# A decoder's fourth norm taken by groups inside the self-attention loop before it, and the first gate group of its feed-forward in halves

## The reference, cut to what matters

```python
def _layernorm(x):                       # no gain, no bias
    return (x - mean(x)) / sqrt(var(x) + 1e-5)

x = x + L0_attn(_layernorm(x));  x = x + L0_xattn(_layernorm(x), ctx);  x = x + L0_ffn(_layernorm(x))
x = x + L1_attn(_layernorm(x))           # 16 heads of 16, relative bias, causal; "second self-attention"
x = x + L1_xattn(_layernorm(x), ctx)     # one head of 256, masked; its norm is "norm 2" here
x = x + L1_ffn(_layernorm(x))

def L1_ffn(x):
    x = act_qdq(x)                       # to 16 bits by the largest |x| of the whole tensor
    up = act_qdq(x @ W_up.T)
    gate = act_qdq(x @ W_gate.T)         # needs the largest |gate| of all 768 x 1600 values first
    sig = fixed_qdq_u16(sigmoid(gate))
    gate = act_qdq(gate * sig)
    return act_qdq(gate * up) @ W_down.T
```

## Time and profile before

| | us |
|---|---|
| median of 3 runs (lowest, highest) | 1400.14 (1398.1, 1403.7) |
| the profiled execution, whole | 1396.8 |
| its span, first to last instruction | 1395.0 |
| PE busy in the span | 1245.3 |
| DVE busy | 1002.9 |
| ACT busy | 748.8 |
| POOL busy | 247.2 |

### The profile page before, as it was taken

The page is one execution under the profiler, slowest core; times in us unless marked ns, Lnnn a source line. Parts: engine busy times, 40 slices in busy tenths (PEclk is TensorE's granted clock), DMA queues, the critical chain, the costliest instruction groups (busy, mean ns, idle before and its releaser), DMA issues.

```text
span 1395.0 us, 27628 instructions
## 1 busy us (share of the span) xinstructions
PE 1245.3 (89%) x9826; PEld 1067.9 (77%) x9826; DVE 1002.9 (72%) x2488; ACT 748.8 (54%) x1769; POOL 247.2 (18%) x330
## 2 busy tenths in 40 slices
PE   5999999979999999999999999999889979979418
PEld 4889989868788777878877788777667756769418
DVE  5975777555677777777777777777689974675984
ACT  5653535354655565555565555565456644425862
POOL 2433323334000000000000000000054433210100
PEclk9999999989999999999999999999999988989859
DMA  9200001041000000000000000000020012300001
GB/s 283 69 1 24 24 3 44 1 165 36 12 1 13 12 12 11 11 0 11 12 11 11 11 0 12 11 1 1 1 61 2 3 47 76 99 26 0 1 0 48
DMA packets 34547, 40.65 MB, mean 29 GB/s; under 512 B 4889, under 2 KB 29066, under 8 KB 34442
## 3 DMA queue, kind: packets, MB, share of 16 engines
q1 hardware_dynamic: 33614, 39.24, 9.1%
q10 hardware_dynamic: 828, 0.14, 0.1%
HBM read 35.36 MB, written 4.01 MB: 28 GB/s over the span
## 4 chain that ended last, share of the span: by engine, by line
PE 52%; DVE 16%; issue 6%; ACT 4%; POOL 1%; DVEq 0%; ACTq 0%; POOLq 0%
PE bank L780 8%; PE bank L782 7%; PE bank L781 7%; PE bank L1003 4%; PE bank L993 3%; PE bank L985 3%; PE bank L961 3%; ACT prob L1679 2%; DVE nmx L2335 2%; DVE amax L2526 2%; PE bank L1237 2%; PE bank L1255 2%; DVE kTl L2106 2%; PE bank L1365 2%; PE bank L1327 1%
## 5 line engine op out<-in xcount | busy, mean ns | idle before, releaser
L1679 ACT ACTIVATE prob<-bank,nmx 100x361 f32<-100x361 f32 x256 | 142.4, 559 | 203.3 <-DVE nmx L2335 199.2
L2335 DVE TENSOR_REDUCE nmx<-bank 100x1 f32<-100x361 f32 x256 | 124.1, 526 | 62.7 <-PE bank L985 61.7
L694 POOL TENSOR_TENSOR frstd<-fmoments,eps 100x1 f32<-100x1 f32 x32 | 6.2, 192 | 645.0 <-DVE fmoments L2278 645.0
L780 PE MATMUL bank<-cxTh,wxkh 128*128 128x362 f32 x256 | 99.9, 390 | 9.4 <-DVE kTl L2106 8.2
L2352 DVE TENSOR_SCALAR prob<-prob,rsum 100x361 f32<-100x361 f32 x256 | 92.9, 405 | 4.5
L993 PE MATMUL bank<-ident,prob 100*128 100x100 f32 (+1 forms) x768 | 89.6, 252 | 0.6 <-DVE prob L2352 0.5
L993 PEld LDWEIGHTS bank<-ident,prob 100*128 100x128 f32 (+1 forms) x768 | 84.5, 151 | 6.2 <-DVE prob L2352 2.0
L780 PE MATMUL bank<-wxvh,cxTh 128*128 128x512 f32 (+1 forms) x192 | 84.5, 440 | 2.0 <-DVE vv L2258 1.6
L782 PE MATMUL bank<-cxTh,wxkl 128*128 128x362 f32 x256 | 84.1, 329 | 0.0
L781 PE MATMUL bank<-cxTl,wxkh 128*128 128x362 f32 x256 | 83.8, 327 | 0.0
L1003 PE MATMUL bank<-pT,vv 128*64 128x100 f32 (+1 forms) x1536 | 81.5, 255 | 1.7 <-ACT pT L1673 0.6
(11 more groups left out here) (428 smaller groups left out, 3686.5 us busy)
## 6 DMA issues: line engine op xcount, KB each, us to landing
cx<-in_ctx_dram SPq DMA_DIRECT2D x32, 128.0 KB, 2.1
xc<-in_ctx_dram SPq DMA_DIRECT2D x32, 128.0 KB
parked_weights<-parking SPq DMA_DIRECT2D x9, 256.0 KB, 5.6
mask_i<-in_mask_BxS_ik_dram SPq DMA_DIRECT2D x16, 141.0 KB
w<-in_L_attn_W_dram SPq DMA_DIRECT2D x2, 1024.0 KB, 13.8
cx<-in_ctx_dram SPq DMA_DIRECT2D x16, 105.0 KB, 2.0
xc<-in_ctx_dram SPq DMA_DIRECT2D x16, 105.0 KB
x<-in_x_dram SPq DMA_DIRECT2D x4, 400.0 KB
```

The source lines that it names most:

```text
L780: pe.matmul(o, wh, mh, start=start, stop=False)
L1679: nc.scalar.activation(prob[:, h % 4, :], bank[S_BANKS[e]][0:T, 0:S], ACT.Exp, bias=nmx[:, h:h + 1], accum_out=psum_[:, h:h + 1]).then_inc ...
L2335: nc.vector.tensor_reduce(nmx[:, h:h + 1], bank[S_BANKS[e]][0:T, 0:S], AX_X, ALU.max, negate=True).then_inc(xa_max, 1)
```

## The change

Norm 2 loses its place behind the loop. A group's work is spread over the iterations behind its last batch: the four `bn_aggr` of groups 0, 1, 2 go to DVE at the end of iterations 5, 9 and 13 (`group_moments`, with a wait for the `bn_stats` just issued); POOL adds the constant and takes the power of -1/2 (`group_deviation`) after its subtractions of iterations 6, 10 and 14; DVE makes minus the mean times that (`minus_means`) at the end of iterations 6, 10 and 14; ACT writes the normalised rows with scale and bias, two batches behind iteration 7 and two behind iteration 8, so for groups 1 and 2 (11, 12 and 15, after the loop) (`half_normalised`). Group 3 has three `bn_aggr` at the loop's end and one after the last batch, POOL's pair after that, and is normalised by DVE inside slot 0 of the cross-attention. PE transposes group 0 between the last transposes and the last weighted sums of iteration 15, group 1 behind those, group 2 behind the last output product, and group 3 inside slot 1 (`rows_transposed`, banks 0, 2, 4 and again 2). The square root on ACT, the reciprocal, and PE's wait for all copies go; before slot 0 PE waits for the copies of groups 0 and 1, in slot 1 for those of group 2.

In the feed-forward `to_all(GATE)` moves from behind up tile 2 to behind up tile 0. ACT calls a sigmoid on one column behind the last gate tile's copy, then copies up tile 0 instead of up tiles 0 to 2, and the first gate group goes through L1859, L1867, L2600 and L2603 in two halves. Two up tiles that were copied before the first gate group are copied behind the second's sigmoid, and two that DVE looked at before the first group are looked at before the third. Counts of the semaphores follow. (The removed `all_deviations`, `all_normalized` and parts of removed functions are left out below; indentation is cut by 8.)

```diff
@@ -418,6 +418,7 @@
 PAIRS = B // 2
+N2_BANKS = (0, 2, 4, 2)
@@ -450,7 +451,7 @@
-TURN = {1: 2 * NG + 4, 2: 2 * NG + 5, 3: 2 * NG + 6}
+TURN = {1: 2 * NG + 4}
@@ -700,6 +701,18 @@
+    def group_deviation(g):
+        nonlocal links
+        links += 1
+        rows = slice(G * g, G * g + G)
+        pool.wait_ge(var_ready, TURN[1] + 2 * g + 1)
+        nc.gpsimd.tensor_tensor(rstd_all[:, rows], moments_all[:, rows, 1], eps[0:T, :].broadcast_to([T, G]),
+                                ALU.add).then_inc(pool_link, 1)
+        pool.wait_ge(pool_link, links)
+        nc.gpsimd.tensor_tensor(rstd_all[:, rows], rstd_all[:, rows], minus_half[0:T, :].broadcast_to([T, G]),
+                                ALU.pow).then_inc(std_ready, 1)
@@ -720,9 +733,11 @@
             rstd_of(2 * B, 1)
-        if b == 2:
             row_with_bias(B - 1)
...
+        if b > 5 and b % G == 2:
+            group_deviation((b - 6) // G)
...
+    group_deviation(NG - 1)
@@ -762,18 +777,14 @@
-    def all_transposes(n):
...
-        for g in range(NG):
-            pe.wait_ge(ln_z, NG * (n - 1) + g + 1)
...
+    def rows_transposed(g):
...
+        pe.wait_ge(ln_z, NG + g + 1)
+        for k in range(KD):
+            for t in range(G):
+                mm = pe.transpose(bank[N2_BANKS[g] + k][:, t * T:(t + 1) * T],
+                                  z[:, G * g + t, k * P:(k + 1) * P], ident[0:T, 0:T])
+            mm.then_inc(ln_t, 1)
@@ -1303,20 +1314,26 @@
             queries_projected(b // 2 + 1)
+        if b == B - 1:
+            pe.wait_ge(a1_sum, 4 * B)
+            rows_transposed(0)
...
             values_projected(b + 2)
+    rows_transposed(1)
     heads_output(B - 1)
-    pe.wait_ge(a1_x, B)
...
-    all_transposes(2)
+    rows_transposed(2)
+    pe.wait_ge(ln_done, KD * NG + 2 * KD)
...
         there, c, o = step(1)
+        if isinstance(g, int) and g == 0 and r == 1:
+            pe.wait_ge(ln_done, KD * NG + 3 * KD)
+            pe.wait_ge(a1_x, B)
@@ -1337,6 +1354,8 @@
         if there and r == 0:
+            if not isinstance(g, int):
+                pe.wait_ge(ln_done, 2 * KD * NG)
@@ -1348,6 +1367,8 @@
                 mm.then_inc(x1_t, 1)
+        if isinstance(g, int) and g == 0 and r == 1:
+            rows_transposed(NG - 1)
@@ -1414,7 +1435,7 @@
             row_transposes(2 if i == 3 else 3)
-        if i == TILES + 2:
+        if i == TILES:
@@ -1468,12 +1485,11 @@
-    def all_copies(n, turn):
-        all_deviations(turn)
-        for g in range(NG):
...
+    def rows_copied_2(g):
...
+        for k in range(KD):
+            act.wait_ge(ln_t, KD * NG + KD * g + k + 1)
+            rows_out(g, k, N2_BANKS[g] + k)
@@ -1776,6 +1792,16 @@
+    def half_normalised(g, half):
...
+        if half == 0:
+            act.wait_ge(var_ready, TURN[1] + 2 * g + 2)
+        for b in range(G * g + 2 * half, G * g + 2 * half + 2):
+            ins = nc.scalar.activation(z[:, b, :], x[:, b, :], ACT.Identity, scale=rstd_all[:, b:b + 1],
+                                       bias=std_all[:, b:b + 1])
+        if half:
+            ins.then_inc(ln_z, 1)
@@ -1797,8 +1823,14 @@
             head_exponents(b + 1)
...
-    all_copies(2, TURN[2])
+        if b > 6 and b % G == 3:
+            half_normalised((b - 7) // G, 0)
+        if b > 6 and b % G == 0:
+            half_normalised((b - 8) // G, 1)
+    half_normalised(NG - 2, 1)
...
+    for g in range(NG - 1):
+        rows_copied_2(g)
@@ -1817,6 +1849,8 @@
             nc.scalar.copy(xcT[:, o, 0, :], bank[0][:, 0:S]).then_inc(x1_ca, 1)
+        if isinstance(g, int) and g == 0 and r == 1:
+            rows_copied_2(NG - 1)
@@ -1849,39 +1883,49 @@
     rows_high(1)
-    for i in range(TILES + 3):
+    for i in range(TILES):
...
             rows_high(2 if i == 3 else 3)
+    nc.scalar.activation(sc[:, 47:48], sc[:, 40:41], ACT.Sigmoid)
+    hidden_out(TILES)
     act.wait_ge(f1_k, 2 * GATE + 1)
-    i = TILES + 3
-    for g in range(NG):
+    i = TILES + 1
+    for half in range(2):
+        of_half = lambda tensor: tensor[:, KI // 2 * half:KI // 2 * (half + 1), 0:N]
+        nc.scalar.activation(of_half(gi), of_half(gt), ACT.Copy, scale=sc[:, 16 + GATE:17 + GATE]).then_inc(f1_gi, 1)
+        act.wait_ge(f1_gi, half + 1)
+        if half == 0:
+            act.wait_ge(f1_k, 2 * GATE + 2)
+        nc.scalar.activation(of_half(gt), of_half(gi), ACT.Sigmoid, scale=sc[:, 24 + GATE:25 + GATE]).then_inc(f1_sig, 1)
+    for _ in range(5):
+        hidden_out(i)
+        i += 1
+    for g in range(1, NG):
         nc.scalar.activation(group(gi, g), group(gt, g), ACT.Copy, scale=sc[:, 16 + GATE:17 + GATE]).then_inc(f1_gi, 1)
-        if g:
-            hidden_out(i)
-            hidden_out(i + 1)
...
+        hidden_out(i)
+        hidden_out(i + 1)
+        i += 2
+        act.wait_ge(f1_gi, g + 2)
         nc.scalar.activation(group(gt, g), group(gi, g), ACT.Sigmoid, scale=sc[:, 24 + GATE:25 + GATE]).then_inc(f1_sig, 1)
-        for _ in range(3 if g else 5):
+        for _ in range(5 if g == 1 else 3):
...
         if g > 1:
-            act.wait_ge(f1_sig, 2 * g - 1)
-            act.wait_ge(f1_p, g - 1)
+            act.wait_ge(f1_sig, 2 * g)
+            act.wait_ge(f1_p, g)
...
             i += 1
+    assert i == 2 * TILES
...
         if g == 0:
-            act.wait_ge(f1_p, NG - 1)
+            act.wait_ge(f1_p, NG)
         if g == 1:
-            act.wait_ge(f1_p, NG)
+            act.wait_ge(f1_p, NG + 1)
@@ -1929,33 +1973,29 @@
-    def all_rows(turn, src=None):
...
-        if src is None:
-            link(nc.vector.memset(pause[:, 3:4], 0.0))
...
+    def row_of(tensor, g, t):
+        return tensor[:, ds(G * g + t, 1), :].rearrange("p a d -> p (a d)")
...
+    def group_moments(g, first, last):
...
+        for b in range(G * g + first, G * g + last):
             ins = nc.vector.bn_aggr(moments_all[:, b, :], stats_all[:, b, :])
-        ins.then_inc(var_ready, 1)
-        dve.wait_ge(std_ready, turn)
-        link(nc.vector.reciprocal(rstd_all[:], std_all[:]))
...
+        return ins
...
+    def minus_means(g):
...
+        rows = slice(G * g, G * g + G)
+        dve.wait_ge(std_ready, TURN[1] + g + 1)
+        nc.vector.scalar_tensor_tensor(std_all[:, rows], moments_all[:, rows, 0], -1.0, rstd_all[:, rows], ALU.mult,
+                                       ALU.mult).then_inc(var_ready, 1)
...
+    def group_normalised(g, first, last):
...
+        dve.wait_ge(std_ready, TURN[1] + g + 1)
+        for b in range(G * g + first, G * g + last):
...
         return ins
...
-    def row_of(tensor, g, t):
-        return tensor[:, ds(G * g + t, 1), :].rearrange("p a d -> p (a d)")
...
-    def norm(n, src=None):
...
@@ -2466,12 +2506,18 @@
         if b:
-            row_stats_1(b - 1)
+            ins = row_stats_1(b - 1)
+        if b > 4 and b % G == 1:
+            link(ins)
+            group_moments((b - 5) // G, 0, G).then_inc(var_ready, 1)
+        if b > 5 and b % G == 2:
+            minus_means((b - 6) // G)
+    link(ins)
+    group_moments(NG - 1, 0, G - 1)
...
     outputs_added(B - 1)
-    row_stats_1(B - 1)
...
-    norm(2)
+    link(row_stats_1(B - 1))
+    group_moments(NG - 1, G - 1, G).then_inc(var_ready, 1)
@@ -2497,6 +2543,8 @@
             nc.vector.tensor_copy(xcT[:, o, 1, :], bank[1][:, 0:S]).then_inc(x1_cd, 1)
+        if isinstance(g, int) and g == 0 and r == 0:
+            group_normalised(NG - 1, 0, G).then_inc(ln_z, 1)
@@ -2595,25 +2643,29 @@
-        if g < 2:
-            dve.wait_ge(f1_sig, g + 1)
+        if g == 1:
+            dve.wait_ge(f1_sig, 3)
...
         else:
-            dve.wait_ge(f1_sig, 2 * g)
+            dve.wait_ge(f1_sig, 2 * g + 1)
...
-        dve.wait_ge(f1_p, g + 1)
+        dve.wait_ge(f1_p, g + 2)
...
-    ups_widest(0, 3)
-    gates_weighted(0)
+    ups_widest(0, 1)
+    for half in range(2):
+        part = slice(KI // 2 * half, KI // 2 * (half + 1))
+        dve.wait_ge(f1_sig, half + 1)
+        link(nc.vector.tensor_scalar(su[:, 0, part], gt[:, part, 0:N], 65536.0, None, ALU.mult))
+        nc.vector.tensor_tensor(gt[:, part, 0:N], gi[:, part, 0:N], su[:, 0, part], ALU.mult).then_inc(f1_p, 1)
     gates_widest(0)
-    ups_widest(3, 8)
+    ups_widest(1, 6)
...
     gates_widest(1)
-    ups_widest(8, 14)
+    ups_widest(6, 14)
```

More of the change, by code:

```diff
@@ L763, in transposes @@
                     mm.then_inc(count, 1)
-            def all_transposes(n):
-                for g in range(NG):
-                    pe.wait_ge(ln_z, NG * (n - 1) + g + 1)
-                    if g >= 2:
-                        pe.wait_ge(ln_done, KD * NG * (n - 1) + KD * (g - 1))
-                    for k in range(KD):
-                        for t in range(G):
-                            mm = pe.transpose(bank[KD * (g % 2) + k][:, t * T:(t + 1) * T],
-                                              z[:, G * g + t, k * P:(k + 1) * P], ident[0:T, 0:T])
-                        mm.then_inc(ln_t, 1)
-                pe.wait_ge(ln_done, KD * NG * n)
```

(42 more changed lines are left out.)

4 lines of the change are left out of this document (removed).

## The result

The changed kernel takes 1391.96 us (median of 6 runs, 1389.07 to 1394.02) against 1399.45 for the kernel before in the same session: ratio 0.9945, 95% interval 0.9931 to 0.996. It is faster, by 7.5 us, where 15.4 were forecast (to 1384.7, with a range of 1380 to 1391). The profiled execution took 1394.0, with a span of 1392.2.

What follows compares the result with a forecast made beforehand. The kernel was taken as mostly PE's (busy 1245 of 1395 us), other engines paying only where PE idles or they carry the end. Norm 12.0 plus gates 3.4 made 15.4, from 1400.1 to 1384.7; whole range 1380 to 1391.

Steps and rivals of the forecast that it cites:

- Part A, what the loop has to carry: Second self-attention's loop: the norm work added on DVE, POOL, ACT and PE costs 0.65 us together, bounds 0.4 and 1.5.
- nothing: POOL in the loop: the added add-and-power pair costs nothing, lying before 3.38 us in which POOL waits for DVE.
- The loop does not hide what it is given: Rival, second self-attention's loop: DVE and ACT pieces and later maxima cost up to 4 us, giving 1388.7; chance 0.10.
- The loop's own cost: DVE in the loop: 0.5 us lost in iteration 13, 0.15 in 14, none in 5 and 9; together 0.65.
- The norm: Loop's end to slot 0's context transposes: ready at 1147.9 instead of 1159.85, 12.0 us gained with the clock held.
- the rivals of the clock's fall: Rival at the loop's end: the clock falls all the same, norm gains 8.4 instead of 12.0, giving 1388.3; chance 0.24.
- of group 3: Rival in the cross-attention: POOL's power or DVE's four rows late for slot 1, 1 to 3 us lost, 1387; chance 0.03.
- of the table loads: Rival in the loop: ACT's Identity reloads a table, eating at most 12.8 us, about no change; chance 0.02.
- of a slower kernel: Rival: the clock falls at the loop's end and stays down through the thinner cross-attention start, slower than before; chance 0.02.
- Part B: Feed-forward's first gate group: earlier to_all, early table load and work in halves gain 3.4 us, bounds 1.8 and 4.6.
- half of it is 2.1: First gate group: DVE's two instructions, 4.14 us, halve to 2.1, so DVE takes the group's largest 4.6 earlier.
- The cover that was named: Third gate group: ACT finishes at 1305.4, 0.4 us before DVE comes at 1305.8; without it the gain sinks to 1.8.

Runs made afterwards that it cites:

- e1: Changed kernel with POOL's output-bias addition to the last row put back in iteration 2 of its loop: 1388.35 us, ratio 0.9911 to the kernel before.
- e2: Kernel before with only POOL's output-bias addition to the last row moved from iteration 2 to iteration 1: 1404.21 us, ratio 1.0029.
- e8: e1 with group 2's bn_aggr, POOL pair and minus_means moved to iteration 15: 1386.37 us, ratio 0.9897 to the kernel before.
- e6: e1 with PE's transposes of groups 0 and 1 put behind the last output product: 1388.43 us, ratio 0.9912 to the kernel before.
- e10: e8 with the first gate group halved by columns of all six tiles instead of by three tiles: 1387.01 us, ratio 0.9909 to the kernel before.
- e11: e8 without ACT's sigmoid on one column, so the table loads at the first sigmoid half: 1388.03 us, ratio 0.9913 to the kernel before.
- e3: Kernel before with only the feed-forward (gates) part of the change: 1401.1 us, ratio 1.0007.
- e9: Kernel before, unchanged, measured and profiled again: 1398.84 us, ratio 0.9991.
- e13: e10 with POOL's last split of the down weights held until DVE's last gate product is done: 1385.27 us, ratio 0.9899 to the kernel before.
- e5: Kernel before with only the norm part, POOL's bias addition to the last row staying in iteration 2: 1388.78 us, ratio 0.9914.
- e4: Changed kernel run and profiled again, unaltered: 1392.69 us, ratio 0.9952 to the kernel before.
- e12: e8 with the gates of the kernel before, so the norm part alone with group 2 late: 1390.06 us, ratio 0.9926 to the kernel before.

## Why the prediction was right or wrong

**The step that failed** stands in "Part A, what the loop has to carry", at POOL: "nothing". It priced the pair that was added to POOL's queue and left out the instruction that the same hunk moves, the bias addition, which changes its iteration when its `if` goes. The time of that instruction (0.72) does not matter; what it waits for does, and what is queued behind it. Of the price some 1.5 came by the clock, which fell behind PE's wait. No rival had any of this. "The loop does not hide what it is given" came nearest, but looked for the loss in iterations 5 to 12. Price: 4.2 (e1, e2).

**Right in kind and size.** The loop's own cost: 0.56 where 0.65 was said, in iterations 13 and 14, and none in 5 and 9 (0.40 between the weighted sums of 13 and 14, 0.16 between those of 14 and 15, under 0.02 anywhere else behind iteration 2); e8 shows that it is these pieces. The norm: 12.2 net where 12.0 was said, with the clock held, no square root and no table load between, the projection in 2.71, group 3 not the chain. ACT's Identity reloads no table: the twelve of the changed kernel (L1800, 0.60 each) have no load among them, and the first load behind 1010 us is the sigmoid's at 1280.51. The prediction and e6's expectation name the clock in GHz; no run shows a frequency. The profiles show a granted clock of 0.50 and 1.00 of full speed, and with them 4.78 and 2.71 for the query projection, 2.04 and 1.11 for the output product, and 1.40 (a quarter of 5.58) and 0.69 for eight transposes. So the rivals of the clock's fall, of group 3, of the table loads and of a slower kernel fall.

**Part B was mis-sized**: 2.1 where 3.4 was said. Two terms. DVE's "half of it is 2.1" took both of its instructions to halve; the scale did not, so DVE took the group's largest 3.4 earlier instead of 4.6, which left 2.4 at the last product; e10 gets 0.85 of it back. Another 0.3 goes at that product, which the earlier start pushes into POOL's subtraction; the cover of 0.43 us that stood there was not looked for. The cover that was named, ACT ahead of DVE at the third group, held (1.1 in the changed kernel: L1917 ended at 1305.3, DVE's product began at 1306.42). The early table, worth 1.28, did all it was said to (e11), and the small sigmoid started 0.01 behind the load's end and took 0.20.

**What was subtracted from.** The sum went from one profiled execution whose clock was at half for 17 us at the norm. Of four profiles with the old norm two had that (the first, e3), one lost 0.85 less (e2) and one 3.47 less (e9), so on average 12 is some 1 too much. Against it, in the kernels with the new norm the half clock at the feed-forward's start lasted 13.7 us instead of 10.2 in part of the profiles, which cost 0.6 to 1.5 between the last context product and the last gate matmul (changed kernel 0.6, e1 1.5, e8 and e13 none; e5 and e11, both with the new norm, 0.9 and 1.2).

**The books.** By stages the changed kernel gains 12.2 + 2.1 - 4.2 - 0.6 = 9.5. The first six runs average 8.2 below the kernel before (plus or minus 1.6, two standard errors; 67 runs of before: mean 1400.0, standard deviation 2.3), e4's twelve 6.8, and all eighteen 7.2, plus or minus 1.3. The reference takes about 1 of the difference; another 1.3 stays, no more than the uncertainty. With the line put back, 12.2 + 2.1 - 1.5 = 12.8, and e1's mean is 12.1 lower, plus or minus 2.5.

**What stays open.** Whether the changed program is always late in the first self-attention (e4). Whether the fillers hold the clock in most executions (e6). And e3: its stage is 2.1 shorter, yet its mean is 0.7 higher than before, plus or minus 1.2. Its trace is 2.4 late at the end of the first self-attention (331 us), as the others are by 0.6 to 7.1, and loses 0.9 in the down projection, as e8 and e11 do (0.8 and 0.9), both in unchanged code; why that should happen in most of its runs was not found. So with the gates alone a gain in device time is not shown. The kernels with the norm part show the gates' worth in the mean (e1 and e8 together 1387.3, e5 and e12 1389.7: 2.4, plus or minus 1.8).

## What to carry to other kernels

When a hunk takes away a condition, list every statement that falls under another one, and for each ask which wait it brings with it and who is queued behind: a wait on a hardly used engine cost more than a third of the norm's gain (4.2 of 12.2), and 1.5 of that was the clock that fell behind it. A half need not cost half: DVE's scale took 1.40 for three tiles of 400, as for all 2400, and 0.78 for six of 200, so look for a row of that very shape. And before a gain is booked downstream, look which engine's work in the other queue lies just ahead of it; DVE's last gate product took 3.78 instead of 2.65 where POOL's subtraction lay beside it for 1.27.

## What the runs showed of the hardware

- DVE's scale of 128x1200 f32 to uint16 took 1.40 us as three tiles of 400 and 0.78 as six of 200; 128x2400 took 1.40.
- DVE's last gate product, 128x2400, took 2.65, 2.96 and 3.78 with 0 (e13), 0.45 (e8) and 1.27 us (e10) of POOL's subtraction beside it. Ten maxima took 4.84 beside the same work of POOL and without it.
- Behind a wait of PE of 2.5 us in iteration 2 the granted clock was at half for 3.4 us in all three profiles with that wait (changed kernel, e4, e2) and in none without it; an output product took 1.91 us in it instead of 1.03.
- The same program's clock fell for 17.1 us in one execution and 6.8 in another at the same place (first profile and e9). Over 67 runs of the kernel before, a us more at half clock went with 0.35 us more of time (time at half clock worked out from each execution's span and mean granted clock).
- Code that no kernel here changes ended its first self-attention 0.6 to 7.1 us later than in the first profile; from there to the start of the second self-attention another -0.2 to 0.3, or about 3, were added.
